# Blockwise FP4 rounding of the gated products: three chunks' lower bound taken by ScalarE, two VectorE steps instead of three

## The reference

```python
def fp4_quant_dequant(x):
    xb = x.reshape(shape[:-1] + (shape[-1] // BLOCK, BLOCK))       # BLOCK = 16
    scale = jnp.maximum(jnp.max(jnp.abs(xb), axis=-1, keepdims=True) / 6.0, 1e-12)
    xn = xb / scale
    idx = jnp.searchsorted(_MID, jnp.abs(xn))
    q = _GRID[idx] * jnp.sign(xn) * scale     # _GRID = 0, 0.5, 1, 1.5, 2, 3, 4, 6
def fp4_linear(x, w):
    return jnp.einsum('bsk,nk->bsn', fp4_quant_dequant(x), fp4_quant_dequant(w))
gate = fp4_linear(x, w_gate)
y = fp4_linear(x, w_up)
h = jax.nn.silu(gate) * y
return fp4_linear(h, w_down)
x = x + _L0_attn_ref(_layernorm(x), ...)
x = x + _L0_ffn_ref(_layernorm(x), ...)
```

## Time and profile before

| what | value |
|---|---|
| median of 3 runs | 1322.12 us (1321.94 to 1322.55) |
| the profiled execution's own time | 1321.53 us |
| its span, first to last instruction | 1319.7 us |
| PE busy | 1255.8 us (95%) |
| DVE busy | 888.1 us (67%) |
| ACT busy | 882.0 us (67%) |
| POOL busy | 1072.5 us (81%) |

### The profile page before, as it was taken

One profiled execution on the slowest core, in us unless ns is written; L12 is line 12 of the kernel. 1 busy time (PEld: TensorE's weight loads), 2 busy tenths in 40 slices (PEclk: granted clock), 3 DMA queues, 4 the chain that ended last, 5 costly groups with the idle time before them and its releaser, 6 DMA issues.

```text
span 1319.7 us, 24786 instructions
## 1 busy us (share of the span) xinstructions
PE 1255.8 (95%) x7417; PEld 658.1 (50%) x7417; DVE 888.1 (67%) x2363; ACT 882.0 (67%) x1246; POOL 1072.5 (81%) x537
## 2 busy tenths in 40 slices
PE   4999999999999999999999999999999998988867
PEld 3555555555455555555455555555555554443336
DVE  6766666677666666677656666677666667675788
ACT  5767676677667676677667676677767666665444
POOL 4488888888888888988888888988888889687767
PEclk9999999999999999999999999999999999999988
DMA  2000000000000000000000000000000000000001
GB/s 64 2 10 1 1 2 10 1 1 1 4 10 1 1 2 10 1 1 2 4 10 1 1 2 10 1 1 2 1 4 1 2 1 1 1 1 1 1 0 33
DMA packets 45953, 6.68 MB, mean 5 GB/s; under 512 B 37344, under 2 KB 45664, under 8 KB 45808
## 3 DMA queue, kind: packets, MB, share of 16 engines
q1 hardware_dynamic: 45584, 4.41, 2.6%
q0 software_dynamic: 224, 0.54, 0.1%
HBM read 3.75 MB, written 1.05 MB: 4 GB/s over the span
## 4 chain that ended last, share of the span: by engine, by line
PE 79%; POOL 8%; DVE 5%; issue 5%; ACT 1%; DMA 1%; SPq 0%; POOLq 0%; DVEq 0%; ACTq 0%
PE o_ps L1323 30%; PE s_ps L1164 23%; PE mx_ps L1186 8%; PE mx_ps L1179 4%; PE misc_ps L1313 3%; PE misc_ps L1301 2%; POOL acc_pool L589 2%; PE misc_ps L1151 2%; POOL acc_pool L588 2%; PE misc_ps L1129 2%; POOL scaled L542 1%; PE s_ps L1172 1%; POOL fx L559 1%; PE misc_ps L1130 1%; PE misc_ps L1131 1%
## 5 line engine op out<-in xcount | busy, mean ns | idle before, releaser
L592 POOL TENSOR_TENSOR acc_pool<-acc_pool,probs 128x1024 f32<-128x1024 f32 x308 | 743.0, 2412 | 46.2 <-POOL acc_pool L592 40.4
L717 ACT ACTIVATE probs<-s_ps 128x1024 f32<-128x1024 f32 x512 | 524.9, 1026 | 80.9 <-PE s_ps L1164 38.6
L901 DVE CUSTOM_DVE_ANT_0 summed<-mx_ps,rise 128x512 bf16<-128x512 f32 x503 | 344.8, 685 | 285.2 <-issue 242.2
L1323 PE MATMUL o_ps<-probs,vv 128*64 128x512 f32 x2048 | 497.4, 606 | 4.3 <-ACT probs L717 4.2
L638 ACT ACTIVATE rise<-mx_ps 128x512 f32<-128x512 f32 x503 | 300.1, 597 | 266.6 <-PE mx_ps L1179 260.5
L1323 PEld LDWEIGHTS o_ps<-probs,vv 128*64 128x64 f32 x2048 | 127.0, 136 | 227.6 <-issue 182.1
L1186 PE MATMUL mx_ps<-k_hi,q_hi 64*128 64x512 f32 x503 | 223.8, 445 | 6.4 <-issue 3.4
L1179 PE MATMUL mx_ps<-k_raw,q_hi 64*128 64x512 f32 x503 | 224.0, 445 | 3.2 <-DVE part_max L901 2.1
L1164 PE MATMUL s_ps<-q_hi,k_hi 64*128 64x512 f32 x1024 | 205.6, 395 | 3.1 <-ACT probs L717 3.1
L1164 PE MATMUL s_ps<-q_hi,k_lo 64*128 64x512 f32 x1024 | 204.3, 392 | 0.0
L1164 PE MATMUL s_ps<-q_lo,k_hi 64*128 64x512 f32 x1024 | 203.8, 391 | 0.0
(11 more groups left out here) (180 smaller groups left out, 1178.7 us busy)
## 6 DMA issues: line engine op xcount, KB each, us to landing
mrow<-neg_max SPq DMA_DIRECT2D x256, 0.5 KB, 2.0
wqkv<-in_L_attn_w_qkv SPq DMA_DIRECT2D x8, 192.0 KB, 2.7
y<-in_L_attn_x SPq DMA_DIRECT2D x4, 256.0 KB, 4.5
out<-y SPq DMA_DIRECT2D x4, 256.0 KB, 2.5
wo<-in_L_attn_w_out SPq DMA_DIRECT2D x8, 64.0 KB, 1.9
wx<-in_L_ffn_w_down POOLq DMA_DIRECT2D x1, 176.0 KB, 5.8
wx<-in_L_ffn_w_gate POOLq DMA_DIRECT2D x1, 128.0 KB, 4.3
wx<-in_L_ffn_w_up POOLq DMA_DIRECT2D x1, 128.0 KB, 5.0
```

What stands on the lines that cost most here:

```text
L592: pool.tensor_tensor(acc, first, probs[:, j % P_BUFS, :, :], ALU.add) \
L717: act.activation(probs[:, j % P_BUFS, :, :], s_ps[:, j % 2, :, :], ACT.Exp, scale=SCALE) \
L901: dve.tensor_tensor_reduce(summed[:, s % 2, :], mx_bank(h, pair), rise[:, h, :], 1.0, LOWEST, ALU.add, ALU.max, part_max[:, slot:slot + 1] ...
L1323: ins = pe.matmul(o_ps[DH * h:DH * (h + 1), :], vv[par(w)][:, j, DH * h:DH * (h + 1)], probs[:, j % P_BUFS, h, :], start=(j == 0), stop=(j ...
```

## The change

For h0, h1 and h2 (n = 5, 6, 7) ScalarE gets a new step "bound n" behind abs n. It writes b = relu(a - 1) and then b = b + 1, which is max(a, 1), to the buffer `split`. Each of the two takes its added constant from a column of a new small buffer `units` and waits for the instruction ahead of it. VectorE's step k = 0 of these chunks goes. Its steps k = 1 and k = 2 become `scalar_tensor_tensor` instructions that multiply b by SPLIT and subtract a in one. Both wait for the bound (`f_bounded`). The weights, the inputs and h3 keep the four steps. GpSimd fills `units` by two memsets at the start of the program.

```diff
@@ ACT_ORDER @@
-             + [("silu", 5), ("sign", 5), ("silu", 6), ("abs", 5), ("silu", 7), ("silu", 8), ("silu", 9), ("T", 3)]
-             + [("sign", 6), ("silu", 10), ("silu", 11), ("abs", 6), ("silu", 12), ("silu", 13), ("ht", 0), ("sign", 7), ("silu", 14)]
-             + [("ht", 1), ("silu", 15), ("abs", 7), ("ht", 2), ("sign", 8), ("ht", 3), ("ht", 4), ("ht", 5), ("abs", 8)]
+             + [("silu", 5), ("sign", 5), ("silu", 6), ("abs", 5), ("bound", 5), ("silu", 7), ("silu", 8), ("silu", 9), ("T", 3)]
+             + [("sign", 6), ("silu", 10), ("silu", 11), ("abs", 6), ("bound", 6), ("silu", 12), ("silu", 13), ("ht", 0), ("sign", 7), ("silu", 14)]
+             + [("ht", 1), ("silu", 15), ("abs", 7), ("bound", 7), ("ht", 2), ("sign", 8), ("ht", 3), ("ht", 4), ("ht", 5), ("abs", 8)]
@@ start of GpSimd's program @@
             in_turn(pool.memset(warm[:, :], 0.0), pool_step)
+            in_turn(pool.memset(units[:, 0:1], -1.0), pool_step)
+            in_turn(pool.memset(units[:, 1:2], 1.0), pool_step)
@@ ScalarE @@
+            def bounded(n):
+
+                a, b = scaled[buf(n)][:, :], split[buf(n)][:, :]
+                act.wait_ge(f_abs, n + 1)
+                act.activation(b, a, ACT.Relu, bias=units[:, 0:1]).then_inc(f_over, 1)
+                act.wait_ge(f_over, n - EARLY)
+                act.activation(b, b, ACT.Identity, bias=units[:, 1:2]).then_inc(f_bounded, 1)
@@ VectorE, grid_step @@
-                if k == 0:
+                if EARLY < n < len(QUANTS) - 1 and k < 3:
+                    settle()
+                    if k == 0:
+                        return
+                    dve.wait_ge(f_bounded, n - EARLY)
+                    if k == 2 and before(n) is not None:
+                        dve.wait_ge(f_quant, quants(before(n) + 1))
+                    inc(dve.scalar_tensor_tensor(a if k == 1 else g, c, SPLIT, a, ALU.mult, ALU.subtract))
+                elif k == 0:
                     dve.wait_ge(f_abs, n + 1 + (part or 0))
                     inc(dve.tensor_scalar(c, a, SPLIT, SPLIT, ALU.mult, ALU.max))
```

More of the change, by code:

```diff
@@ L182, in block_kernel @@
         warm = sb("warm", [P, 2])
+        units = sb("units", [P, 2])
         amax = sb("amax", [P, 2, TQ * FF // BLOCK])
@@ L307, in block_kernel @@
         f_abs = sem("f_abs")
+        f_over = sem("f_over")
+        f_bounded = sem("f_bounded")
         f_grid = sem("f_grid")
@@ L750, in _ @@
                     signs(n)
+                elif what == "bound":
+                    bounded(n)
                 elif what == "abs":
```

## The result

Over twelve runs each the changed kernel took 1325.18 us in the median (1323.11 to 1332.05), the kernel before 1322.03 us (1320.25 to 1324.99). The ratio is 1.0029 with a 95% interval of 1.0020 to 1.0039, so 2.6 to 5.2 us slower. Timed again on another occasion it was 1.0020 (1.0008 to 1.0033), 2.6 us. The forecast was 1326.1 us, slower by 0.3%, in a range of 1323.0 to 1328.6.

A forecast was written before the change was run, and what follows sets the result against it. In the tail it took ScalarE's in-order queue, with silu 7 waiting only for its place, as the bound. Shifts of +3.0 at tile 7 and +4.0 from tile 12 on gave 1325.5, as median 1326.1 us, range 1323.0 to 1328.6.

The forecast's parts named there:

- The price of a pair: ScalarE's two instructions for one bound: 3.0 us with hand-offs, between 2.65 and 3.3 us.
- The new VectorE steps: VectorE's two scalar_tensor_tensor steps per chunk: kept at the old mean of 1.875 us, at most 0.1 us more each.
- Place 1, tile 7: VectorE's product of tile 7: silu 7 comes after the first pair, so +3.0 us.
- Place 2, tile 12: VectorE's product of tile 12: +4.0 us by ScalarE's path, which comes later than VectorE's own at about +1.8.
- over 6: GpSimd's step ahead of abs 6 and the second pair: taken as 6.43 us, perhaps up to 0.6 us longer.
- new wait for silu 12: Sign of being right: VectorE newly waits some 2 us for silu 12.
- Place 3, tiles 12 to 15: Stage paced by products, TensorE and silu: line 832's absence brings nothing, so the shift stays +4.0 us.
- longer slow stretch: Rival, 14%: longer waits before gu 9 and gu 14 prolong TensorE's low clock, giving 1327.9 us.
- Place 4, third pair: Pair behind abs 7 delays sign 8 and later steps: first half of h3 +3.4 to +4.3 us, taken as +4.0.
- Places 5 and 6: From the half of h3 to the output as before, so still +4.0 us; the two memsets at the start hidden.
- VectorE as the bound of the stretch: Rival, 9%: ScalarE fits the pairs into idle time, only line 832's removal counts, 3.4 us faster, 1318.7 us.
- The hidden second pair: Rival, 15%: GpSimd's over 6 takes 3.2 instead of 6.4 us, leaving some +1.6 us, 1323.7 us.

The follow-up runs named there:

- e8: The change for h0 alone, its pair ahead of silu 7, h1 and h2 as in the kernel before: ratio 1.0025 to the kernel before.
- r1: The changed kernel timed and profiled again, nothing edited: ratio 1.0020 to the kernel before, tail 54.84 us.
- e10: The changed kernel without the third pair, so h2 has neither pair nor fused steps: ratio 1.0020 to the kernel before, tail 55.54 us.
- e1: The kernel before with only the new buffer and its two memsets added: ratio 1.0002, tail 50.59 us.
- e2: The kernel before with ScalarE's three pairs added, VectorE keeping its four steps: ratio 1.0032, tail 54.58 us.
- e3: The changed kernel without pairs, VectorE's fused steps reading the divided values: ratio 0.9963 to the kernel before, 0.9983 when timed again.
- e6: The changed kernel with bound and fused steps for h0 alone, its pair between silu 8 and silu 9: ratio 0.9999 to the kernel before.

## Why the prediction was right, step by step

Direction, size and mechanism held; the sum's later terms were off, and that it came out near is partly luck, since errors cancelled.

- *The price of a pair.* 3.0 us forecast, 2.90 us measured. Each instruction took 1.47 us against the estimate of 1.48 from line 655. The Trainium skill, ScalarE: Activation LUTs, "What ACT_TABLE_LOAD costs", gives 0.28 us plus 0.833 ns a column with a constant from a column, an estimate of 1.45 us; the trace agrees.
- *The new VectorE steps.* Kept at 1.875 us; they took 1.60 to 2.10 us, in the mean 1.87 and 1.79 us.
- *Place 1, tile 7:* +3.0 forecast, +3.00 measured.
- *Place 2, tile 12:* +4.0 forecast, +3.42 measured. The mis-sized term is over 6, 5.78 instead of 6.43 us. I had it longer at most, or as short as 3.2 us in a rival; that its second piece, without line 832 beside it, would run ahead of VectorE's first fused step was not in the sum. The same order holds up that step, so VectorE's own path came at +2.34 (e8) and not at +1.8, and the new wait for silu 12 is 1.00 us, not some 2.
- *Place 3, tiles 12 to 15:* 0 forecast. The wait ahead of gu 14 grew by 1.14 us, not by 2 to 3. The shift was 0 where the clock rose in time (profile after), +1.3 us where it didn't (r1). I gave the longer slow stretch 14%. The profiles show it in four of the six with 3.35 us of waiting ahead of gu 14, so that was too low.
- *Place 4, third pair:* I had the first half of h3 between +3.4 and +4.3, level with place 3; it came at +2.43 in the profile after, 1.0 us less than its tile 15. This step failed. (Its lower end is 0.2 us too high by its own terms: 1302.83 + 4.0 - 0.87 is 1305.96, not 1306.2.) The third pair ended at 1304.40, just ahead of the reciprocals at 1304.63 for which sign 8 would have waited anyway, so sign 8 came 0.1 us late and not 0.4. The detour over ht 4 and ht 5, for which I allowed up to 0.6 us, cost nothing: sign 8 started at +3.52 us and abs 8 at +3.15. With 0.75 us of slack this gives +2.4. In r1 sign 8 stood at +4.81 and abs 8 at +4.82, and the half of h3 at +4.10: inside my range, but only because gu 15 had been slow. The comparison of e10 and r1 shows the same small price of the third pair.
- *Sum:* +4.0 forecast for the tail, +2.53 and +4.1 in its two profiles, 3.8 and 2.6 us in the two ratios. In the profile after, place 4 (1.0 us) and over 6 (0.6 us) were overrated. In r1 over 6 (0.6 us) and place 4 (0.6 us) stood against an underrated clock (1.3 us), so that its +4.1 meets the forecast by luck. Places 5 and 6 held: from the half of h3 to the end it is 14.1 us before, 14.2 and 14.1 after, and e1 shows no price for the start.
- *The rivals.* VectorE as the bound of the stretch falls with e2, and with e3, which gives 2.4 us even without any pair. The hidden second pair falls: over 6 would have had to be 3.2 us.

Left open: what makes the low clock last into gu 15, and how often it does so in unprofiled runs.

## What to carry to other kernels

An engine that is busy half the time is no free engine: what counts is the place in its order, and who waits for the instruction behind. The two instructions cost 3.0 us in front of a silu that VectorE was waiting for. Behind the next two silus they cost nothing at tile 7 and up to 0.9 us at tile 12, because one product 0.1 us late let GpSimd go ahead of VectorE. Moved to the waits, the change gains 1.2 us of tail in one profile instead of losing 2.5, though no ratio here tells it from the kernel before. Before work is moved from a full engine to a half-idle one, look for the idle time on the receiving engine's timeline, put the work in it, and check that the full engine is really what comes last in each stage; here that held for the rounding of h0 (1.55 us without pairs), for that of h1 not at all, and for that of h2 up to the slack at abs 8 (0.7 us).

## What the runs showed of the hardware

- TensorE ran at 1.2 GHz from about 35 to 55 us in one profile of the changed kernel, in the first 15 us of it while busy without a gap (0.50 granted, 5.00 of 5.00 us busy), and in the second profile of the same kernel not at all. From 0.9 us ahead of the kernel before the profile fell to 6.8 us behind in that stretch.
- A start 0.12 us later on VectorE (e6 against e3, behind GpSimd's next piece instead of ahead of it) lengthened the instruction by 0.62 us. In all seven profiles in which this step starts inside that piece it ends 1.48 or 1.49 us behind the piece's end.
- A step that waits for the one ahead of it on ScalarE starts 0.03 us after its end; independent ones start 0.10 us ahead of it.
